# The product with V as three 256-column matmuls per key block instead of a 512- and a 256-column one

## What is computed

```
def attn(x):                        # x is layernorm(x)
    Q = x @ Wq.T + bq; K = x @ Wk.T + bk; V = x @ Wv.T + bv
    scores = einsum('bqd,bkd->bqk', Q, K) / sqrt(d) * gaussian_mask
    return einsum('bqk,bkd->bqd', softmax(scores), V) @ Wo.T + bo
x = x + attn(layernorm(x))
x = x + ffn(layernorm(x))           # ffn: gelu(x @ bw1.T + b1) @ bw2.T + b2, bw binarized
```

## Time and profile before

| | |
|---|---|
| runs | 1577.24, 1578.99, 1581.0 us; median 1578.99 |
| the profiled execution, first to last instruction | span 1576.1 us |
| PE busy | 1553.5 us (99%), 9421 matmuls |
| PEld busy | 1366.9 us (87%), 9421 weight loads |
| DVE busy | 1167.2 us (74%), 2034 instructions |
| ACT, POOL busy | 654.8 us (42%), 484.5 us (31%) |
| mean granted TensorE clock | 0.998 |

### The profile page before, as it was taken

How to read it: one execution, slowest core, us unless ns; L and a number is a source line. 1 busy time by engine, 2 the same in 40 slices (tenths; PEclk the granted TensorE clock), 3 DMA queues, 4 the chain that set the end, 5 groups by cost and what they waited for, 6 DMA issues and landing times.

```text
span 1576.1 us, 24294 instructions
## 1 busy us (share of the span) xinstructions
PE 1553.5 (99%) x9421; PEld 1366.9 (87%) x9421; DVE 1167.2 (74%) x2034; ACT 654.8 (42%) x838; POOL 484.5 (31%) x713
## 2 busy tenths in 40 slices
PE   8999999999999999999999999999999999999998
PEld 6888888898888888888888888889888888888887
DVE  8685867858678586885858768586785867858676
ACT  4452443624335253352533535334352443624333
POOL 4133151332413333132421423314133151333314
PEclk9999999999999999999999999999999999999999
DMA  4001001010000101001010010100101000010000
GB/s 154 1 1 54 1 15 42 1 54 1 29 28 1 54 1 55 1 1 54 1 56 1 3 52 1 56 1 14 41 1 56 1 21 34 1 54 1 28 1 27
DMA packets 10046, 39.31 MB, mean 25 GB/s; under 512 B 942, under 2 KB 3260, under 8 KB 7996
## 3 DMA queue, kind: packets, MB, share of 16 engines
q1 hardware_dynamic: 9888, 37.49, 6.2%
q10 hardware_dynamic: 28, 0.01, 0.0%
HBM read 20.72 MB, written 16.78 MB: 24 GB/s over the span
## 4 chain that ended last, share of the span: by engine, by line
PE 81%; DVE 14%; issue 2%; ACT 1%; DMA 1%; SPq 0%; POOL 0%; POOLq 0%; DVEq 0%
PE ps L712 20%; PE ps L733 15%; PE ps L735 8%; PE ps L722 7%; DVE gl L521 7%; PE ps L748 6%; PE ps L749 6%; PE ps L887 5%; DVE gh L519 5%; PE ps L690 2%; PE ps L699 2%; PE ps L700 2%; PE ps L702 2%; PE ps L687 2%; PE ps L688 2%; PE ps L757 2%
## 5 line engine op out<-in xcount | busy, mean ns | idle before, releaser
L372 ACT ACTIVATE pth<-ps 128x1024 fp32r<-128x1024 f32 x128 | 131.2, 1025 | 418.1 <-PE ps L722 418.1
L733 PE MATMUL ps<-vhl,pth 128*128 128x512 f32 x1024 | 268.7, 404 | 0.0
L748 PE MATMUL ps<-sgn,gh 128*128 128x256 f32 x1024 | 241.5, 281 | 0.9 <-DVE ys L528 0.4
L367 ACT ACTIVATE prob<-ps,nmax 128x1024 f32<-128x1024 f32 x128 | 142.1, 1111 | 233.8 <-PE ps L749 229.3
L749 PE MATMUL ps<-sgn,gl 128*128 128x256 f32 x1024 | 238.8, 279 | 0.0
L250 POOL TENSOR_TENSOR ve<-mv,eps 128x1 f32<-128x1 f32 x128 | 24.3, 190 | 669.3 <-DVE mv L505 669.3
L477 DVE TENSOR_REDUCE nmax<-ps 128x1 f32<-128x1024 f32 x128 | 156.6, 1224 | 92.7 <-PE ps L712 92.7
L733 PEld LDWEIGHTS ps<-vhl,pth 128*128 128x128 f32 x1024 | 182.9, 188 | 34.4
L482 DVE TENSOR_TENSOR ptl<-ps,pth 128x1024 fp32r<-128x1024 f32 x128 | 156.7, 1224 | 68.6 <-ACT pth L372 68.6
L748 PEld LDWEIGHTS ps<-sgn,gh 128*128 128x128 f32 x1024 | 192.9, 188 | 5.6 <-DVE ys L528 3.5
L749 PEld LDWEIGHTS ps<-sgn,gl 128*128 128x128 f32 x1024 | 192.9, 188 | 0.6
(11 more groups left out here) (112 smaller groups left out, 2774.9 us busy)
## 6 DMA issues: line engine op xcount, KB each, us to landing
out_dram<-xin SPq DMA_DIRECT2D x32, 512.0 KB, 2.6
xin<-in_L_attn_x_dram SPq DMA_DIRECT2D x15, 1024.0 KB, 4.9
xin<-in_L_attn_x_dram SPq DMA_DIRECT2D x2, 512.0 KB, 4.8
w1s<-in_L_ffn_w_dram SPq DMA_DIRECT2D x1, 1024.0 KB, 10.3
w2s<-in_L_ffn_w_dram SPq DMA_DIRECT2D x1, 1024.0 KB, 12.4
mask_bc<-mask_dram SPq DMA_DIRECT2D x1, 512.0 KB, 7.3
wk<-in_L_attn_Wk_dram SPq DMA_DIRECT2D x1, 256.0 KB, 5.5
wq<-in_L_attn_Wq_dram SPq DMA_DIRECT2D x1, 256.0 KB, 6.1
```

Of the source, the lines that this page charges most:

```text
L367: act.activation(two(prob[:, q % 2, :]), slot(q % 2), ACT.Exp, bias=nmax[:, q:q + 1], accum_out=rsum[:, q:q + 1]).then_inc(exp_set, 1)
L372: act.activation(two(pth[:, q % 2, :]), ps[:, PT_BANK:PT_BANK + 2, :], ACT.Copy).then_inc(pth_set, 1)
L733: pe.matmul(bank, pth[:, q % 2, tile(t)], vhl[:, t, :, :], start=t == 0, stop=False)
L748: pe.matmul(bank, gh[:, j, tile(t)], sgn2[:, j, :], start=j == 0, stop=False)
```

## The change

The product with V no longer uses one 512-column matmul per key block. Two 256-column matmuls with the same stationary operand take its place, one with `vh` and one with `vl`, and both add into columns 0 to 255 of the bank. The low·high matmuls stay as they were. The sum of the three products is then complete in PSUM, and the DVE instruction that added columns 256 to 511, with its semaphore `x1_half` and the wait for it, goes. Nothing else differs. Line numbers of the changed file are three lower behind L493 and two lower behind L735.

```
                 dve.wait_ge(xbias_added, T * b + q + 1)
-                dve.scalar_tensor_tensor(out=xin[s][:, q, :], in0=ps[:, OUT_BANK + q % 2, D:2 * D], scalar=rinv[:, q:q + 1],
-                                         in1=xin[s][:, q, :], op0=ALU.mult, op1=ALU.add).then_inc(x1_half, 1)
-                dve.wait_ge(x1_half, T * b + q + 1)
                 dve.scalar_tensor_tensor(out=xin[s][:, q, :], in0=ps[:, OUT_BANK + q % 2, 0:D], scalar=rinv[:, q:q + 1],
                                          in1=xin[s][:, q, :], op0=ALU.mult, op1=ALU.add).then_inc(x1_set, 1)
...
-                bank = ps[:, OUT_BANK + q % 2, :]
+                bank = ps[:, OUT_BANK + q % 2, 0:D]
                 for t in range(T):
-                    pe.matmul(bank, pth[:, q % 2, tile(t)], vhl[:, t, :, :], start=t == 0, stop=False)
+                    pe.matmul(bank, pth[:, q % 2, tile(t)], vh[:, t, :], start=t == 0, stop=False)
+                    pe.matmul(bank, pth[:, q % 2, tile(t)], vl[:, t, :], start=False, stop=False)
                 for t in range(T):
-                    last = pe.matmul(bank[:, 0:D], ptl[:, q % 2, tile(t)], vh[:, t, :], start=False, stop=t == T - 1)
+                    last = pe.matmul(bank, ptl[:, q % 2, tile(t)], vh[:, t, :], start=False, stop=t == T - 1)
```

More of the change, by code:

```diff
@@ L162, in preln_attention_ffn @@
             sem(n) for n in ("q_summed", "qh_set", "ql_set", "v_summed", "vh_set", "vl_set"))
-        scored, max_set, exp_set, p_turned, pth_set, ptl_set, rinv_set, pv_summed, x1_half, x1_set = (
+        scored, max_set, exp_set, p_turned, pth_set, ptl_set, rinv_set, pv_summed, x1_set = (
             sem(n) for n in ("scored", "max_set", "exp_set", "p_turned", "pth_set", "ptl_set", "rinv_set",
-                             "pv_summed", "x1_half", "x1_set"))
+                             "pv_summed", "x1_set"))
         stats2, aggr2, vareps2, rstd2_set, xn2_set, b2_added = (
```

## The result

The changed kernel is slower, by a little more than the measurement can tell from nothing: 1581.97 us median against 1578.91 us, 18 runs of each, a ratio of 1.0021 with a 95% interval of 1.0013 to 1.0029. The profiled execution has a span of 1580.7 us, 4.6 us more than the one of before.

A forecast was written before the change was run, and what follows sets the result against it. PE streaming its columns was taken to bound the kernel: span 1576.1 - 6.2 (columns on PE) + 0 (DVE add) = 1569.9 us, plus 2.9 us from span to median, so 1572.8 us; range 1568.0 to 1584.0 us.

The forecast's parts named there:

- Part 1, the DVE add at 0: Attention part: removing 60.8 us of DVE adds, none on the path, gains 0, with -0.5 us as bound.
- Part 2, the columns on PE: Product with V on PE: same columns, 1024 more matmuls, today 367.8 us; forecast change -6.2 us.
- The slow bound: Product with V, all new streams slow: 2.91 us a tile behind transposes, 371.0 us in all, 3.2 us more.
- I take `values` as it is: Product with V takes the speeds of `values`: 13/16 fast at -8.4 us, 3/16 slow at +3.2 us, giving -6.2 us.
- The bound of all fast: Product with V, all new streams fast: 2.82 us a tile behind transposes, 359.4 us in all, 8.4 us less.
- The weight loads at nothing: Product with V on PE: 1024 extra weight loads cost nothing, covered by the stream itself, as in `ffn_rows`.
- The fixed part for each matmul: PE: the skill's gap of N/2.4 + 2.5 ns would add 2.6 us for 1024 more matmuls; dismissed.
- Slow streams: Rival, product with V: the new stream settles at the slow speed, 3.2 us more, 1582.2 us; chance 0.20.
- Carried-over slow streams: Rival: slow new streams also slow `values` and the hidden layer, 6.1 us on top, 1588.3 us; chance 0.10.
- a sign that it is wrong: Feed-forward part: the prediction is wrong if PE's stalls there change with the new speed of the stages ahead.
- Columns alone: Rival, product with V: columns cost their present average however cut, within 1.5 us of nothing, 1579 us; chance 0.20.
- the step from span to time: Whole kernel: the median of runs lies 2.9 us above the profiled span, so 1569.9 us becomes 1572.8 us.

The follow-up runs named there:

- The grouped order: Changed kernel with a tile's 24 matmuls in three groups of eight, never the same stationary operand twice in a row: 1582.63 us, ratio 1.0034 against the kernel before.
- second profile of before: The kernel before, unchanged, profiled once more: span 1577.6 us, hidden layer at 14.94 us in 10 of 15 batches.
- placing the operands: Kernel before with four pads putting 512-column operand pairs at distance 0 modulo 512 bytes, 256-column ones at 320: 1577.04 us, ratio 0.9996.
- scores cut: Kernel before with the scores cut into 24 matmuls of 256 columns per tile, product with V as before: 1593.39 us, ratio 1.0079.

## Why the prediction was wrong

**What bounds the kernel.** Right for this change. PE's stream sets the time; a cut on PE moves it and 61 us less on DVE do not. It was not the whole of it: with GpSimd's adds moved, which takes the stalls out of `ffn_rows` and shortens the wait at the end, the kernel is 4.3 us faster (1574.91 against 1579.23 us).

**Part 1, the DVE add at 0.** Right: 1.0005 (0.9995 to 1.0016) with that half alone. No new wait appeared.

**Part 2, the columns on PE.** The frame was right: the number of columns stays, the distance between starts decides, there are two speeds, and today's 367.8 us were 367.4. The slow bound was right too: 2.91 us a tile was put down and 2.91 was measured. **The step that failed is the choice between them**, "I take `values` as it is", 13/16 at -8.4 us. `values` was the nearest row by its entry behind transposes and its repeated stationary operand. The grouped order showed that the second likeness has no weight. The second profile of before showed that the share was a draw: `values` was fast in 12 passes of one execution and in 5 of the next. (The prediction counts 13. The first pass, of 5.82 us, is a slow one at 118 ns a matmul.) I read the share of a speed in one execution as a property of the code. The term measured +2.1 us instead of -6.2. The row that was put aside, L735 at 118 ns in 13 batches of 16, pointed the right way only by luck: in the second profile it is fast in 11 of 16. No row of before shows what the runs showed in place of the mixture, lone tiles that are slow in 97 of 98 cases. The bound of all fast was not reached in any batch either, and the part of it that came, the fast pair, came with slow `values` and a slow hidden layer.

**The weight loads at nothing.** Right only as far as no load makes PE wait for it. In starts they were not free everywhere: at distance 0 a 256-column matmul takes 120 ns and a 512-column one 227. Whether it is the second load that costs the difference, no run shows by itself.

**The fixed part for each matmul.** I dismissed the 2.5 ns of the Trainium skill ("TensorE: Matmul & The Clock Gate", section "Back-to-back issue gap") because 228 was twice 113. Both numbers are real, but they come from operands at different distances, 0 and 320. At one distance the trace shows 227 against 2 x 120 and 233 against 2 x 113 or 2 x 118. So no one fixed part fits, but its 2.6 us for 1024 more matmuls are near the 2.1 us that the product with V lost.

**The rivals.** *Slow streams* was what happened: 1582.2 us forecast, 1581.97 measured, at a chance of 0.20. That the two lie so close is luck: the product with V lost 2.1 and 1.9 us in the two pairs of profiles and not 3.2, because pairs were fast. *Carried-over slow streams* had the tie but turned it round: it is the fast pair that comes with slow `values` and a slow hidden layer. More batches were slow outside the product, but that varies by itself, and their loss is in part paid back by fewer stalls in `ffn_rows` (6 batches of 15 with one, 12 before). The prediction had named such a change of the stalls as a sign that it is wrong. I had priced a stage without asking what waits behind it. *Columns alone* was near, at 1579.

**The range** held the time. The chances did not fit: 0.50 on faster rested on one execution's draw. So did part of the step from span to time, taken as 2.9 us: the runs on record lie some 1.8 us above their own spans, and the rest is a profiled execution faster than the median.

**Still open** is why the lone tiles behind transposes take 118 ns nearly always while `values` behind transposes takes either. The order and the region of PSUM were excluded, the stage ahead was excluded as the sole cause, and what is left was not found. So the price of the change is shown to lie in the cut on PE, but why the new stream settles at its slow speed is not shown.

## What to carry to other kernels

A 512-column matmul is not two 256-column ones for free. In this kernel of float32r matmuls a cut cost 2 to 3 ns in the lone tiles of the product with V and 10 to 13 at distance 0; only where the halves ran at 113 ns, in the pair of tiles of some batches, did it gain, and the stages behind lost more. It buys nothing where the engine that it relieves has slack. Where PE streams without a hole, look at the distance between starts for each stage and batch, and profile the same program twice before a share of fast and slow batches goes into a sum. A gain in one stage is only worth what the next wait leaves of it: placing the operands gave nothing until GpSimd's adds were moved off DVE's path, which alone gave 0.25%, and then the two together gave 0.65%.

## What the runs showed of the hardware that was not expected

**The distance in SBUF between stationary and moving operand changes the rate of matmuls**, though PE has nothing else to wait for. All rows are float32r at the full granted clock, ns from start to start:

| distance modulo 512 bytes | 256 columns | 512 columns |
|---|---|---|
| 0 | 120 (product with V, scores cut) | 227 (hidden layer, scores), 228 or 231 (product with V) |
| 64 | 118 (low parts) | 233 (hidden layer) |
| 128 | 118.6 (`values`) | 232 (hidden layer) |
| 160 | - | 234 (hidden layer) |
| 192 | - | 229 or 233 (hidden layer) |
| 256 | - | 228 or 231 (product with V) |
| 320 | 113 or 118 (`values`, `ffn_rows`, product with V) | 233 (product with V) |
| 352, 384 | 119 (product with V) | - |
| 448 | 118 (product with V), 113 or 118 (`values`) | - |

Places 256 bytes apart agree where there are two to compare (0 and 256 for 512 columns in the product with V; 64 and 320 for 512 columns, and at 118 for 256; 128 and 384), so the period may be 256; 113 ns, seen at 320, was not seen at 64 in one execution, and the runs do not settle it. The Trainium skill says that the loading of weights does not take read bandwidth from the running matmul ("TensorE: Matmul & The Clock Gate", section "Step-by-step: what each phase is for") and that PE never waits on other engines' ports ("SBUF — State Buffer", section "SBUF: two separate sides"). The rows here bear on the first alone, and it does not account for them: a pad of 64 bytes, with no instruction changed, cost the changed kernel some 12 us or 0.7% (1593.73 against 1581.97 us). That the loads are what collides was not shown by itself, and no run separates it from what the other engines read and write in the tiles that were moved.

**Two speeds at one distance.** A stream of 256 columns at 320 bytes runs at 113.3 or at 117.8 ns a matmul, and `values` keeps one of the two through a pass of 48. A stall can turn one into the other: `ffn_rows` of before begins at 118 ns, has its stall in 12 of 15 batches and goes on at 113 ns in 9 of these, while the 3 batches without a stall stay at 118. In the same program the hidden layer was slow in 3 batches of 15 in one execution and in 10 in the next, and the spans differed by 1.5 us. Fast and slow are not free of each other: in the 165 batches of the 11 profiles that have the distances of the kernel before, a fast pair of tiles (or L735) came with slow `values` and a slow hidden layer, and a slow pair with both fast, in all but 2 batches of the kernel with cut scores.
